# First pair of an eight-pair Strassen kernel: new orders on all engines, scalings in turn, product 2 by tile of the contraction, projections a group later

## The reference

```
q_emb = relu(cond @ W3 + b3)                       # 16 x 1024
y     = relu(((512*x + sum_t x) * q_emb) @ W2 + b2)  # first layer
base  = y @ W_base + b_base
gates = softmax(y @ W_router + b_router); the two largest of 6 are kept, the rest 0
low   = (y @ A_s) @ B_s + sum_e gate_e * (y @ A_r[e]) @ B_r[e]
out   = x + base + low
```

## Time and profile before

| | |
|---|---|
| median of 3 runs | 1448.36 us (1447.81 to 1448.74) |
| the profiled execution: its time, its span | 1448.76 us, 1446.7 us |
| busy share of the span: PE, PEld, DVE, ACT, POOL | 99%, 81%, 63%, 47%, 3% |
| mean granted clock of TensorE | 0.996 |

### The profile page before, as it was taken

How to read it: one execution, slowest core, us unless ns; L and a number is a source line. 1 busy time by engine, 2 the same in 40 slices (tenths; PEclk the granted TensorE clock), 3 DMA queues, 4 the chain that set the end, 5 groups by cost and what they waited for, 6 DMA issues and landing times.

```text
span 1446.7 us, 18245 instructions
## 1 busy us (share of the span) xinstructions
PE 1429.2 (99%) x6314; PEld 1168.9 (81%) x6314; DVE 905.4 (63%) x1540; ACT 677.9 (47%) x1303; POOL 39.7 (3%) x71
## 2 busy tenths in 40 slices
PE   9889999999999999999999999999999999999999
PEld 5668888888888888888888888888888888888887
DVE  6966566564755647557788756565555646665564
ACT  6674674847658576585543232232322313132230
POOL 3130000000000000000000000000000000000000
PEclk9999999999999999999999999999999999999999
DMA  8231322413234232343653627246171542717242
GB/s 307 88 124 52 127 92 94 132 68 114 88 103 132 73 108 82 102 138 131 208 200 119 246 66 247 95 158 212 46 277 59 181 183 79 256 66 237 106 141 93
DMA packets 107229, 196.30 MB, mean 136 GB/s; under 512 B 12160, under 2 KB 12160, under 8 KB 107136
## 3 DMA queue, kind: packets, MB, share of 16 engines
q1 hardware_dynamic: 107136, 195.13, 39.8%
HBM read 123.78 MB, written 71.30 MB: 135 GB/s over the span
## 4 chain that ended last, share of the span: by engine, by line
PE 93%; DVE 3%; ACT 1%; issue 0%; POOL 0%; DVEq 0%; ACTq 0%
PE ps L1376 31%; PE ps L1378 31%; PE ps L1377 31%; DVE act_lo L930 1%; PE ps L1508 0%; DVE w_lo L916 0%; ACT src L575 0%; PE ps L1502 0%; DVE buf L975 0%; DVE src L962 0%; POOL w_hi L522 0%; DVE buf_lo L1010 0%; DVE wl_raw L1153 0%; DVE r L1135 0%; DVE src L968 0%
## 5 line engine op out<-in xcount | busy, mean ns | idle before, releaser
L1376 PE MATMUL ps<-act_hi,w_hi 128*128 128x512 f32 x1792 | 702.2, 392 | 4.2 <-issue 4.2
L1378 PE MATMUL ps<-act_hi,w_lo 128*128 128x512 f32 x1792 | 698.6, 390 | 0.0
L1377 PE MATMUL ps<-act_lo,w_hi 128*128 128x512 f32 x1792 | 698.4, 390 | 0.0
L1376 PEld LDWEIGHTS ps<-act_hi,w_hi 128*128 128x128 f32 x1792 | 337.1, 188 | 76.0 <-issue 5.0
L1378 PEld LDWEIGHTS ps<-act_hi,w_lo 128*128 128x128 f32 x1792 | 337.0, 188 | 70.7
L1377 PEld LDWEIGHTS ps<-act_lo,w_hi 128*128 128x128 f32 x1792 | 337.0, 188 | 69.0
L607 ACT ACTIVATE act_hi<-src 128x512 fp32r<-128x512 f32 x380 | 233.5, 623 | 258.5 <-PE ps L1378 256.8
L930 DVE TENSOR_TENSOR act_lo<-src,act_hi 128x512 fp32r<-128x512 f32 x320 | 220.3, 692 | 128.7 <-ACT act_hi L607 127.7
L975 DVE SCALAR_TENSOR_TENSOR buf<-ps,bb_sb,buf 128x512 f32<-128x512 f32 x128 | 95.7, 749 | 164.7 <-PE ps L1378 149.3
L975 DVE SCALAR_TENSOR_TENSOR buf<-ps,b_sb,buf 128x512 f32<-128x512 f32 x96 | 71.7, 749 | 66.2 <-PE ps L1378 65.8
L626 ACT ACTIVATE yhi<-buf 128x512 fp32r<-128x512 f32 x128 | 79.9, 625 | 39.1 <-PE ps L1378 38.9
(11 more groups left out here) (113 smaller groups left out, 997.1 us busy)
## 6 DMA issues: line engine op xcount, KB each, us to landing
src<-in_xT SPq DMA_DIRECT2D x224, 256.0 KB, 2.9
y_scratch<-buf SPq DMA_DIRECT2D x128, 256.0 KB, 2.1
src<-y_scratch SPq DMA_DIRECT2D x128, 256.0 KB, 5.1
outT<-buf SPq DMA_DIRECT2D x128, 256.0 KB, 4.3
buf<-in_xT SPq DMA_DIRECT2D x32, 256.0 KB, 4.5
wl_raw<-in_wbase SPq DMA_DIRECT2D x6, 1024.0 KB, 5.9
r<-in_w SPq DMA_DIRECT2D x16, 256.0 KB, 7.9
wh_raw<-in_wbase SPq DMA_DIRECT2D x3, 1024.0 KB, 8.1
```

The costliest lines, as they stand in the source:

```text
L1376: nc.tensor.matmul(out, wh, a_h, start=start, stop=False, skip_group_check=onto)
L1377: nc.tensor.matmul(out, wh, a_l, start=False, stop=False, skip_group_check=onto)
L1378: return nc.tensor.matmul(out, wl, a_h, start=False, stop=stop, skip_group_check=onto)
```

## The change

All of it concerns the first pair.

- ScalarE scales G12 and G22 tile by tile in turn, and puts `high` of product 2 between; `x1_no` gives the new count of the semaphore. It then makes `a_hi`, which GpSimd made before. The rest of its order up to product 5 is new: two `relu` instead of four before `high` of product 3, `copy_u4` and `y_high` elsewhere, `relu` of tiles 2 and 3 last.
- VectorE makes all of product 2's `w_lo` before t1, then t1 and t2 of a tile together. Two of the four `c11` move behind product 4's work, as do t3 and t4 of tiles 1 to 3. It makes `a_lo`. `y_low` of C11's tiles 2 and 3 moves ahead of product 5's `low`.
- GpSimd loses `a_hi` and `a_lo`; the shift for pair 1's G12 moves ahead of product 5's casts, and each cast waits for its own s3 sum instead of all four.
- TensorE runs product 2 by tile of the contraction, and each `project_y` from product 4 on one group later; the last one comes after product 6.
- SP stores C11's tiles 2 and 3 after it has issued the loads of the next G12 and G22.

Two waits that only change their count (`x1_no` in t1 and t2) and the branch for `i > 0`, moved but the same, are cut here.

```diff
@@ -274,6 +274,12 @@
+        def x1_no(i, q, k):
+            if i == 0 and q != G21:
+                return H + 2 * k + (G12, G22).index(q) + 1
+            return tile_no(i, q, k)
         def y_no(i, c, j):
@@ -357,14 +363,17 @@
+            def store_c11(i, j):
+                sp.wait_ge(relu_done, four(i, j))
+                sp.dma_start(y_dram[2 * i, j], buf1[:, j, :]).then_inc(buf1_stored[j], 16)
             def pair(i):
                     load_quadrant(wl_raw[:, 0], Q11, wl_loaded[0])
-                for j in range(H):
-                    sp.wait_ge(relu_done, four(i, j))
-                    sp.dma_start(y_dram[2 * i, j], buf1[:, j, :]).then_inc(buf1_stored[j], 16)
+                for j in range(H if i > 0 else 2):
+                    store_c11(i, j)
                     if j == 1 and i > 0:
@@ -381,6 +390,9 @@
                     store_hw(i - 1, GA)
+                else:
+                    store_c11(0, 2)
+                    store_c11(0, 3)
                 for k in range(H):
@@ -537,14 +549,10 @@
                 w2_high(3, s12, k)
-            pool.wait_ge(a_loaded, 16)
-            nc.gpsimd.tensor_copy(a_hi[:], a_raw[:]).then_inc(a_hi_made, 1)
-            pool.wait_ge(a_hi_made, 1)
-            nc.gpsimd.tensor_tensor(a_lo[:], a_raw[:], a_hi[:].bitcast(F32), ALU.subtract).then_inc(a_made, 1)
-            for k in range(H):
-                pool.wait_ge(s3_made, H)
+            shift_of(1, G12)
+            for k in range(H):
+                pool.wait_ge(s3_made, k + 1)
                 w2_high(5, r21, k)
-            shift_of(1, G12)
             for k in range(H):
@@ -567,9 +575,9 @@
-            def x_scale(i, q):
+            def x_scale(i, q, ks=range(H)):
                 act.wait_ge(shift_made, source_no(i, q) + 1)
-                for k in range(H):
+                for k in ks:
                     t = tile(q, k)
@@ -598,7 +606,7 @@
                 elif g < NP:
-                    act.wait_ge(x1_ready, tile_no(g, {0: G11, 1: G21, 4: G22}[n], k))
+                    act.wait_ge(x1_ready, x1_no(g, {0: G11, 1: G21, 4: G22}[n], k))
                 else:
@@ -704,8 +712,14 @@
                 copy_p0(0, j)
-            x_scale(0, G12)
-            x_scale(0, G22)
+            for k in range(H):
+                x_scale(0, G12, (k,))
+                x_scale(0, G22, (k,))
+                if k > 0:
+                    high(0, 2, k - 1)
+            high(0, 2, H - 1)
+            act.wait_ge(a_loaded, 16)
+            nc.scalar.activation(a_hi[:], a_raw[:], ACT.Copy).then_inc(a_hi_made, 1)
             act.wait_ge(bias_loaded, 16 * 4)
@@ -738,42 +752,56 @@
                     copy_p0(i, H - 1)
-                for j in range(H):
-                    high(i, 2, j)
-                    if i > 0 and j > 0:
-                        relu(i, j - 1)
                 if i == 0:
-                    for j in range(H - 1):
-                        relu(i, j)
-                for j in range(H):
-                    high(i, 3, j)
-                    if j == 0:
-                        relu(i, H - 1)
-                    else:
-                        copy_u2(i, j - 1)
-                    if j == 1 and i > 0:
-                        copy_h(i - 1, GA)
-                    if last:
-                        wb_high(0, j)
-                if i > 0:
-                    exponent(i - 1, GA)
-                else:
+                    relu(0, 0)
+                    relu(0, 1)
+                    for j in range(H):
+                        high(0, 3, j)
+                    for j in range(H):
+                        copy_u2(0, j)
                     for k in range(H):
-                        act.wait_ge(s4_made, H)
+                        act.wait_ge(s4_made, k + 1)
                         act.wait_ge(w2_lo_done, 2 * H + k + 1)
                         nc.scalar.activation(w_hi[:, 4, k, :], r12[:, k, :], ACT.Copy).then_inc(s4_hi_done, 1)
-                copy_u2(i, H - 1)
-                for j in range(H):
-                    high(i, 4, j)
-                    if j > 0:
-                        copy_u4(i, j - 1)
-                    if j >= 2:
-                        y_high(i, C11, j - 2)
-                    if not last:
-                        x_sum(i + 1, G12, j)
-                    else:
-                        wb_high(1, j)
-                copy_u4(i, H - 1)
+                    for k in range(H):
+                        high(0, 4, k)
+                    copy_u4(0, 0)
+                    for k in range(H):
+                        x_sum(1, G12, k)
+                    y_high(0, C11, 0)
+                    for j in range(1, H):
+                        copy_u4(0, j)
+                    y_high(0, C11, 1)
+                    relu(0, 2)
+                    relu(0, 3)
+                else:
...
+                    copy_u4(i, H - 1)
                 if not last:
@@ -1099,12 +1127,9 @@
                 nc.vector.tensor_tensor(s2[:, k, :], s12[:, k, :], r11[:, k, :], ALU.subtract).then_inc(s2_made, 1)
-            w2_low(2, s2, (0, 1))
+            w2_low(2, s2)
             for k in range(H):
                 t1(0, k)
-                if k >= 2:
-                    w2_low(2, s2, (k,))
-            for k in range(H):
                 t2(0, k)
@@ -1114,26 +1139,34 @@
             def first_pair():
-                for j in range(H):
-                    c11(0, j)
+                c11(0, 0)
+                c11(0, 1)
                 w2_low(3, s12)
+                for j in range(H):
+                    low(0, 3, j)
                 for k in range(H):
                     nc.vector.tensor_tensor(r12[:, k, :], r12[:, k, :], s2[:, k, :], ALU.subtract).then_inc(s4_made, 1)
-                for j in range(H):
-                    low(0, 3, j)
-                for j in range(H):
+                t3(0, 0)
+                t4(0, 0)
+                w2_low(4, r12)
+                for j in range(H):
+                    low(0, 4, j)
+                dve.wait_ge(a_hi_made, 1)
+                nc.vector.tensor_tensor(a_lo[:], a_raw[:], a_hi[:].bitcast(F32), ALU.subtract).then_inc(a_made, 1)
+                for j in range(1, H):
                     t3(0, j)
                     t4(0, j)
-                w2_low(4, r12)
-                for j in range(H):
-                    low(0, 4, j)
                 y_low(0, C11, 0)
+                c11(0, 2)
+                c11(0, 3)
                 y_low(0, C11, 1)
                 w2_low(5, r21)
+                y_low(0, C11, 2)
+                y_low(0, C11, 3)
@@ -1203,7 +1236,7 @@
                     low(i, 5, j)
-                    if j in (1, 2):
+                    if i > 0 and j in (1, 2):
                         y_low(i, C11, j + 1)
@@ -1463,6 +1496,7 @@
+                onto = n in ONTO
                 for k in range(H):
@@ -1470,8 +1504,9 @@
                         cols = slice(j * P, (j + 1) * P)
-                        mm = three(ps[:, j if n == 0 else Z_BANK + j, :], w_hi[:, n, k, cols], w_lo[:, n, k, cols],
-                                   act_hi[:, slot(0, n, k), :], act_lo[:, slot(0, n, k), :], k == 0, k == H - 1)
+                        mm = three(ps[:, Z_BANK + j if n == 1 else j, :], w_hi[:, n, k, cols], w_lo[:, n, k, cols],
+                                   act_hi[:, slot(0, n, k), :], act_lo[:, slot(0, n, k), :], k == 0 and not onto,
+                                   k == H - 1, onto)
                         if k == H - 1:
@@ -1510,8 +1545,8 @@
                 if i == 0:
-                    first_groups(0)
-                    first_groups(1)
+                    for n in range(3):
+                        first_groups(n)
                 else:
@@ -1522,23 +1557,25 @@
                             turn_gates(i - 1, GB)
-                for j in range(H):
-                    group(i, 2, j)
-                    if j == 2 and i > 0:
-                        turn_h(i - 1, GA)
+                    for j in range(H):
+                        group(i, 2, j)
+                        if j == 2:
+                            turn_h(i - 1, GA)
                 for j in range(H):
                         turn_gates(i - 1, GA)
-                for j in range(H):
-                    group(i, 4, j)
-                    project_y(i, C11, j)
-                for j in range(H):
-                    group(i, 5, j)
-                    project_y(i, C12, j)
-                for j in range(H):
-                    group(i, 6, j)
-                    project_y(i, C22, j)
+                tiles = [(c, j) for c in (C11, C12, C22) for j in range(H)]
+                late = int(i == 0)
+                for n in (4, 5, 6):
+                    for j in range(H):
+                        group(i, n, j)
+                        at = H * (n - 4) + j - late
+                        if at >= 0:
+                            project_y(i, *tiles[at])
+                if late:
+                    project_y(i, *tiles[-1])
```

(55 more changed lines are left out.)

## The result

The changed kernel takes 1440.69 us (median of 6 runs, 1440.28 to 1441.32) against 1448.55 for the kernel before beside it (1447.81 to 1449.6): 0.9946 of its time, 95% interval 0.9933 to 0.9958, so 7.9 us less. The forecast was 1439.8. A second measurement on another chip gave 1441.01 against 1449.27.

A forecast was written before the change was run, and what follows sets the result against it. TensorE bounds the kernel, with 14.6 us of idle and half clock to win and 6.1 given back: 8.5, or 8.65 by end points. Taking 8.6 off 1448.36 gave 1439.8, own range 1438 to 1442, with near rivals 1435.5 to 1443.5.

The forecast's parts named there:

- 14.6: TensorE's idle and half clock after product 1: 3.16 + 1.88 + 1.40 + 6.17 + 2.0 us, everything the change can win.
- 6.1: Part of the gain given back: 0.4 before product 2; 1.3, 1.4 and 3.0 us before and in product 5.
- Products 3 and 4 are hidden: VectorE's operands come ahead of need, by about 1.2 us at product 3 and 1.9 at product 4.
- GpSimd's turns: GpSimd and VectorE alternate: about 1.02 us per cast and subtraction, 1.70 per turn with a GpSimd subtraction.
- The one step that failed: At product 2, the clock fell after 3.2 and 6.2 us idle, not 1.4, so no half clock was booked.
- The fall: Rival: the clock falls again between 73.9 and 83, costing about 2.0 us, for 1441.8; chance 0.17.
- run through: Rival: from product 5's first low on VectorE shuts GpSimd out, winning 3.0 us more, for 1436.8; chance 0.2.
- The price of that, 3.0: In product 5's first group, three quarters of 0.68 us each wait for a turn of 1.70: 3 x 1.0 idle.
- the gain goes at product 5: Rival: VectorE's 14 instructions each take the worst turn, 1.70 us, for 1448.4; chance 0.06 for over 1445.5.
- the slower case: Rival: VectorE's queue from 44.3 to 66.45 takes 1.02 per turn, fourth C11 15 us late, for 1454.9; chance 0.03.
- 3.16 and 1.88 at product 2: TensorE's idle before product 2, 3.16 us, and half clock inside it, 1.88; only 0.39 idle was to stay.

The follow-up runs named there:

- e9: The changed kernel with ScalarE scaling all of G12, then all of G22, then copying product 2's four tiles, as before the change; 1442.97 us, ratio 0.9957.
- e3: The changed kernel, but GpSimd begins product 6's casts and subtractions only after product 5's fourth low, with pair 1's G22 shift between them; 1437.25 us, ratio 0.9917.
- e1: The changed kernel with product 2 of the first pair by group again, all else as changed; 1441.79 us, ratio 0.9946.
- e5: The changed kernel with product 2 by group and each projection right behind its own group, as before the change; 1441.70 us, ratio 0.9949.
- e8: The changed kernel with the cast and subtraction of the projection matrix back on GpSimd, behind product 3's casts; 1442.37 us, ratio 0.9955.
- e7: The changed kernel with GpSimd's shift for pair 1's G12 back behind product 5's casts; 1444.93 us, ratio 0.9970.
- e6: The changed kernel with GpSimd's product 6 work after product 5's low, two low before C11's last y_low, and both TensorE orders undone; 1439.23 us, ratio 0.9930.
- e2: The changed kernel with each projection of the first pair right behind its own group, as before the change; 1441.55 us, ratio 0.9947.

## Why the prediction was right

**The sum.** The losses (idle and half clock) from the end of product 1 to the second group of product 5 are 14.75 before (39.47 to 92.30, 38.08 of work) and 7.1 after (39.73 to 84.93); the prediction had 14.6 and 6.1. Its steps, forecast and measured: product 2 starts at 39.86 and 39.82; third projection 75.15 and 75.20; product 5 77.2 and 77.28; second quarter 78.9 and 78.93; then 80.6 and 80.61, 82.3 and 82.29. Products 3 and 4 are hidden as said, `a_lo` took 1.21 (1.2), GpSimd's turns are 1.02 and 1.7.

**The one step that failed** is "The clock fell after stretches of 3.2 and 6.2 idle and not after 1.4, so I book no half clock", where it was carried to product 5. The fall was a rival there, at 0.17 and 2.0 us. It fell, at 78.0 in both profiles of the changed kernel, and cost less than 2.0, since three quarters hid part of it. From the third projection's start to the second group of product 5 the changed kernel takes 9.7 us (75.20 to 84.93), and e9, which has the same waits and full clock, takes 8.6 (80.04 to 88.6). This 1.1 is the difference between 6.1 and 7.1 in the profiles. It is about the 0.9 between 1439.8 and 1440.7 as well, but only two executions of the changed kernel have a profile, both with the fall; the fastest, 1440.28 with a mean clock of 1.00, is still 0.5 over the forecast.

**The rivals.** VectorE didn't run through: every `low` took its turn. The price of that, 3.0, was right as a part: from the third projection's start to the second group of product 5 e3 takes 5.6 instead of 9.7 us, 3.0 of it the turns and 1.1 the clock. That the gain goes at product 5 was right in place and wrong in size, and the slower case had nothing to it: VectorE's queue from 44.3 to 66.4 kept its 0.60, but for the four `w_lo` beside the last casts (3.32 for 2.48, forecast too). What such a stream costs GpSimd was overlooked: it kept the shift for pair 1 from 59.56 to 65.23, and the scalings that need it start at 67.06. That they weren't late is luck, by a margin of 1.8 that the prediction hadn't counted.

**What the prediction didn't say** is how the parts share the gain. Its sum books each stall where it stood: 3.16 and 1.88 at product 2, which it lets start early by the scalings in turn and by the order by tile. e1 shows that the order by tile has no part in the early start. TensorE's two orders together give 0.7 by the medians, inside the noise (e5). The gain is in VectorE's unbroken queue, which e9 (1.6 to 2.0) and e8 (1.0 to 1.4) lengthen, and in the shift ahead of the casts (e7: 3.6 to 4.0). These three are parts undone one by one and need not add up. Not tried alone: the move of two `c11`, t3 and t4 after product 4's operands, product 5's first cast after one sum, and the new order of ScalarE and of the stores.

## What to carry to other kernels

When several stalls of the busiest engine hang on one chain of another engine, follow that chain, not the stalls: removing an early stall only feeds the late one, until the chain itself is shorter. Ask of every instruction on GpSimd whose VectorE instructions stand beside it, and put GpSimd's work where VectorE has nothing due; here that and a few moved splits won 5.5 us more than the change. A wait's printed releaser that ended long before is the sign to look for the semaphore that really came last.

## What the runs showed of the hardware

A 4-column product on GpSimd (the shift) that takes 0.2 to 0.65 us elsewhere took 5.67 (59.56, rows above), while VectorE ran two-operand subtractions without a gap. It ended when VectorE came to its two additions from PSUM:

```profile
65.09 1.40 DVE L1003 SCALAR_TENSOR_TENSOR buf<-ps,b_sb,buf 128x512 f32<-128x512 f32 x2
```

In all eleven profiles that have the shift there (all but that of e7) it ended 0.14 or 0.15 us after these additions began, wherever it had started: in e1 it ran from 61.06 to 64.85 with the additions at 64.71, in e8 from 62.44 to 66.97 with them at 66.83. So here VectorE's unbroken stream shut GpSimd out for as long as it lasted. Where VectorE came to such an instruction while GpSimd was already at work, the two took turns to the end: at 45.66 beside the casts of product 3 (3.32 for 2.48) and from 70.01 to 82.2. The Trainium skill (SBUF — State Buffer, Who interferes with whom) tells of an exclusive lock held for a whole instruction. The turns of 1.02 and 1.70 us agree with it; the 5.67 us over a whole stream is what these runs show. Why the one happens and not the other isn't shown.

The granted clock fell without long idle, and not each time. In the changed kernel it fell after idle pieces of 1.2 and 1.3 us with three matmuls between, in both profiles; with the same pieces it stayed at full in e9. In e5 it fell inside product 2 after two pieces of 1.1 us with three matmuls between, and with the same pieces it stayed at full in e1 and e6. In e2 one piece of 2.1 was enough (0.51 from 67.5 to 71).
